# Moving the max pieces, the projections, the turned maxima and the weighted sums to other slots of a software-pipelined cross-attention

## What is computed

```python
q = (query @ Wq + bq).reshape(B, Nq, H, D).transpose(0, 2, 1, 3)        # B=32, Nq=56, H=16, D=8
k = (key_value @ Wk + bk).reshape(B, Nkv, H, D).transpose(0, 2, 1, 3)   # Nkv=1500
v = (key_value @ Wv + bv).reshape(B, Nkv, H, D).transpose(0, 2, 1, 3)
attn = jnp.einsum('bhqd,bhkd->bhqk', q, k) * scale
attn = jax.nn.softmax(jnp.clip(attn, -CLAMP, CLAMP), axis=-1)
x = jnp.einsum('bhqk,bhkd->bqhd', attn, v).reshape(B, Nq, Cq)
return x @ Wo + bo
```

## Time and profile before

| what | before |
|---|---|
| median of three runs | 974.03 us |
| profiled execution: time | 974.64 us |
| profiled execution: span | 972.5 us (2.1 us lie around it) |
| TensorE matmul busy | 924.9 us, 95% |
| VectorE / ScalarE / GpSimd busy | 699.5 / 645.9 / 351.0 us |

### The profile page before, as it was taken

The page is one execution under the profiler, slowest core; times in us unless marked ns, Lnnn a source line. Parts: engine busy times, 40 slices in busy tenths (PEclk is TensorE's granted clock), DMA queues, the critical chain, the costliest instruction groups (busy, mean ns, idle before and its releaser), DMA issues.

```text
span 972.5 us, 28783 instructions
## 1 busy us (share of the span) xinstructions
PE 924.9 (95%) x10471; PEld 741.4 (76%) x10471; DVE 699.5 (72%) x1490; ACT 645.9 (66%) x1081; POOL 351.0 (36%) x332
## 2 busy tenths in 40 slices
PE   6777999999999999999999999999999999999995
PEld 4655777777777777777777777777777778999894
DVE  6673777767676677676767767767788857777996
ACT  4654777777777777777777777777776545445554
POOL 6452362222333333222233333332222413112992
PEclk8897999999999999999999999999999999999998
DMA  5538566666655555666666555566665201002321
GB/s 141 121 79 191 120 133 140 143 136 137 137 128 119 119 119 126 141 137 138 136 137 134 119 119 119 120 137 143 137 138 111 69 1 44 23 23 86 128 114 41
DMA packets 43626, 111.44 MB, mean 115 GB/s; under 512 B 15491, under 2 KB 26053, under 8 KB 43461
## 3 DMA queue, kind: packets, MB, share of 16 engines
q1 hardware_dynamic: 43572, 110.77, 50.3%
HBM read 32.23 MB, written 1.89 MB: 35 GB/s over the span
## 4 chain that ended last, share of the span: by engine, by line
PE 84%; ACT 5%; DVE 4%; issue 3%; SPq 2%; POOL 1%; DMA 1%; ACTq 0%; DVEq 0%; POOLq 0%
PE psum L1592 17%; PE psum L1424 16%; PE psum L1652 13%; PE psum L1431 8%; PE psum L1436 8%; PE psum L1656 4%; ACT arena L759 3%; PE psum L1679 2%; PE psum L1692 2%; PE psum L1691 2%; PE psum L1680 2%; PE psum L1681 2%; PE psum L1693 2%; PE psum L1441 1%; SPq L396 1%
## 5 line engine op out<-in xcount | busy, mean ns | idle before, releaser
L946 DVE TENSOR_REDUCE arena<-psum 128x1 f32<-128x500 f32 x672 | 447.8, 674 | 210.1 <-PE psum L1424 206.9
L759 ACT ACTIVATE arena<-psum 125x896 f32<-125x896 f32 x384 | 347.5, 916 | 109.0 <-PE psum L1592 101.7
L1424 PE MATMUL psum<-K_hi,Q_bd 128*128 128x500 f32 x672 | 319.6, 485 | 7.0 <-DVE arena L946 4.1
L547 POOL TENSOR_TENSOR arena<-arena,K_hi 128x500 fp32r<-128x500 f32 x96 | 120.7, 1257 | 403.3 <-ACT K_hi L690 403.3
L1592 PEld LDWEIGHTS psum<-Q_st,K_st 97*125 97x125 f32 x1536 | 221.6, 189 | 42.4 <-ACT arena L759 16.6
L1592 PE MATMUL psum<-Q_st,K_st 97*125 97x224 f32 x1536 | 238.6, 278 | 6.1 <-ACT arena L759 5.6
L1652 PE MATMUL psum<-arena 125*25 125x168 f32 x3072 | 170.5, 311 | 0.2
L1424 PEld LDWEIGHTS psum<-K_hi,Q_bd 128*128 128x128 f32 x672 | 128.6, 192 | 53.3 <-issue 20.8
L813 ACT ACTIVATE K_st<-psum 128x448 fp32r<-128x448 f32 x128 | 69.8, 545 | 79.5 <-PE psum L1681 78.0
L1656 PE MATMUL psum<-arena 125*9 125x56 f32 x3072 | 117.6, 213 | 0.0
L1656 PEld LDWEIGHTS psum<-arena 125*9 125x9 f32 x3072 | 94.1, 91 | 16.6
(11 more groups left out here) (249 smaller groups left out, 983.3 us busy)
## 6 DMA issues: line engine op xcount, KB each, us to landing
K_st<-K_hi SPq DMA_DIRECT2D x256, 187.5 KB, 4.8
K_st<-arena SPq DMA_DIRECT2D x128, 187.5 KB, 3.4
arena<-in_ctx SPq DMA_DIRECT2D x32, 562.5 KB, 6.8
arena<-gate_rows SPq DMA_DIRECT2D x8, 896.0 KB, 4.4
arena<-in_L_ffn_W SPq DMA_DIRECT2D x16, 256.0 KB, 3.2
Q_st<-max_row SPq DMA_DIRECT2D x224, 0.5 KB, 1.7
arena<-OS_all SPq DMA_DIRECT2D x12, 168.0 KB, 4.0
x_rows<-x_all SPq DMA_DIRECT2D x1, 896.0 KB, 6.4
```

The source lines that it names most:

```text
L547: g.tensor_tensor(low.bitcast(F32R), low, K_hi[:, par, n * KB:n * KB + KB].bitcast(F32), ALU.subtract).then_inc(F["keys_low"], 1)
L759: a.activation(P2[c % NP].rearrange("p (n k) -> p n k", n=2), psum[0:CK, 2 + 2 * (c % 2):4 + 2 * (c % 2), 0:HQ // 2], ACT.Exp)\
L946: v.reduce_max(mx[:, n // NB, n % NB:n % NB + 1], bank_of(n)[:, 0:KB], AX.X).then_inc(F["piece_max_taken"], 1)
L1424: mm(bank_of(n)[:, 0:KB], Q_bd[:, par].rearrange("p h q -> p (h q)")[:, 128 * (n // NB):128 * (n // NB) + 128], K_hi[:, par, (n % NB) * KB ...
```

## The change

It writes new numbers into the slot tables and makes some of what they imply explicit. Ten pieces of batch b+2 run ahead instead of nine (`NEXT`). T moves from slot 8, behind p0, to slot 9, behind p3 and V0 (`BEFORE_TURN` = 4: p0 to p3 of batch b+2 now stand ahead of T, so the bank parity of pieces is shifted, T also waits for the maximum of p2, and p5 rather than p2 waits for `row_out`). V2 moves from slot 3 to 1, K0 to K2 from slots 5, 6, 8 to 4, 5, 6. The weighted sums move from slots 2, 5, 8, 10, 11 (2+3+3+1+3) to 3, 5, 8, 10, 11 (2+3+2+2+3). On VectorE the five steps of the softmax sums move from slots 0 to 4 to slots 3 to 5. The maxima `mx` get one buffer per parity, since p0 of the next batch now may be reduced before `row_max` has run. In the prologue four pieces of batch 1 stand ahead of `turn(0)`, and three of their maxima ahead of `row_out(0)`.

```diff
-V_SLOTS = (9, 11, 3)
-K_SLOTS = (5, 6, 8)
-SUM_SLOT, TURN_SLOT = 0, 8
-K_COPIES = (4, 6, 7)
...
+V_SLOTS = (9, 11, 1)
+K_SLOTS = (4, 5, 6)
+COPY_SLOT, SUM_SLOTS, SCALE_SLOT = 0, (3, 3, 4, 5), 5
+ROW_SLOT, TURN_SLOT, KEEP_SLOT = 7, 9, 9
+V_COPIES = (9, 11, 2)
+K_COPIES = (3, 5, 6)
+NEXT, BEFORE_TURN = 10, 4
...
         def bank_of(n):
 
-            return bank[0 if n == 0 else (n + 1) % 2]
+            return bank[(n + (n >= BEFORE_TURN) + 1 + BEFORE_TURN) % 2]
...
-            row_max(0)
+            row_max(0, 0)
+            for n in range(BEFORE_TURN - 1):
+                piece_max(1, 1, n)
             row_out(0)
-            for n in range(3):
-                piece_max(1, n)
+            for n in range(max(BEFORE_TURN - 1, 0), BEFORE_TURN + 2):
+                piece_max(1, 1, n)
...
-                if n == 2:
+                if n == BEFORE_TURN + 1:
                     if turns:
                         pe.wait_ge(F["max_row_ready"], b + PRIME)
...
-            def turn(b):
+            def turn(b, more):
 
                 pe.wait_ge(F["row_max_taken"], b + 1 + PRIME)
+                if more and BEFORE_TURN > 1:
+                    pe.wait_ge(F["piece_max_taken"], (b + 1) * PIECES + BEFORE_TURN - 1 + PRIME)
...
-            pieces1(0)
-            turn(0)
-            pieces1(1)
+            pieces1(*range(BEFORE_TURN))
+            turn(0, True)
+            pieces1(BEFORE_TURN)
```

More of the change, by code:

```diff
@@ L329, in pieces @@
         def pieces(c, table):
-            return [(2 if n < 9 else 1, n) for n in table.get(c, ())]
+            return [(2 if n < NEXT else 1, n) for n in table.get(c, ())]
         def bank_of(n):
-            return bank[0 if n == 0 else (n + 1) % 2]
+            return bank[(n + (n >= BEFORE_TURN) + 1 + BEFORE_TURN) % 2]
         def has(b, ahead):
@@ L749, in period @@
                 for c in range(NC):
-                    if c == 0 and has(b, -1):
+                    if c == COPY_SLOT and has(b, -1):
                         act.wait_ge(F["outputs_made"], b * NC + PRIME)
@@ L760, in period @@
                          .then_inc(F["weights_ready"], 1)
-                    if c == 9 and has(b, 1):
+                    if c == KEEP_SLOT and has(b, 1):
                         keep_extremes(b + 1)
@@ L988, in _, with taken @@
             v.memset(bank[6], 0.0).then_inc(F["bank_cleared"], 1)
-            for n in range(3, 9):
-                piece_max(1, n)
-            def taken(b, c, table):
+            for n in range(BEFORE_TURN + 2, NEXT):
+                piece_max(1, 1, n)
+            def taken(b, par, c, table):
                 for ahead, n in pieces(c, table):
@@ L995, in taken @@
                         continue
-                    piece_max(b + ahead, n)
+                    piece_max(b + ahead, (par + ahead) % 2, n)
             def period(b, par, half):
                 for c in range(NC):
[L1000 to L1003, removed]
+                    taken(b, par, c, EARLY_PIECES)
+                    taken(b, par, c, MID_PIECES)
+                    if c == ROW_SLOT and has(b, 1):
+                        row_max(b + 1, 1 - par)
                     if c == TURN_SLOT and has(b, 1):
@@ L1534, in _, with bank_free @@
             last.then_inc(w_ps, 1)
-            pieces1(2, 3)
+            pieces1(*range(BEFORE_TURN + 1, BEFORE_TURN + 3))
             pe.wait_ge(F["keys_copied"], 2 * NB + PRIME)
             value_project(1, 0)
-            pieces1(4, 5, 6, 7)
+            pieces1(*range(BEFORE_TURN + 3, NEXT - 1))
             pe.wait_ge(F["values_copied"], NB + 1 + PRIME)
             value_project(1, 1)
-            pieces1(8)
+            pieces1(NEXT - 1)
+            def bank_free(b, kind, n):
+                if isinstance(b, int) and b == B - 2:
+                    pe.wait_ge(F["keys_copied"], B * NB + PRIME)
+                    pe.wait_ge(F["values_copied"], B * NB - 1 + PRIME)
+                    return
+                i = [p[1:] for p in PROJECTIONS].index((kind, n))
+                if isinstance(b, int) and b == 0 and i == 0:
+                    pe.wait_ge(F["values_copied"], NB + 2 + PRIME)
+                _, last, m = PROJECTIONS[i - 1]
+                batch = 1 if last == "values" and m == 2 else 2
+                pe.wait_ge(F[f"{last}_copied"], b * NB + ((batch - (i == 0)) * NB + m + 1) + PRIME)
             def max_scores(b, par, c, table):
@@ L1624, in period @@
                         n = V_SLOTS.index(c)
-                        if n == 0:
-                            pe.wait_ge(F["keys_copied"], (b + 3) * NB + PRIME)
-                        else:
-                            pe.wait_ge(F["values_copied"], b * NB + (ahead * NB + n) + PRIME)
+                        bank_free(b, "values", n)
                         value_project((par + ahead) % 2, n)
```

66 lines of the change are left out of this document (32 added, 34 removed).

## The result

The changed kernel is slower: 993.72 us in the median of four runs (991.71 to 999.82) against 974.50 of the kernel before (972.60 to 975.99, four runs), a ratio of 1.021 (95% interval 1.016 to 1.026). I had forecast 985 (974 to 993): the direction is right, the size is 9 us short and just outside the range. The profiled execution is the longest of the four, 999.82 us with a span of 998.0, so its spans hold some 6 us more than the median.

A forecast was written before the change was run, and what follows sets the result against it. TensorE's own order was taken to bound the steady loop. Loop +1.5, slow row DMAs +2.5, start +4.5 and end +2.5 summed to +11 on a profiled 974.64: 985.6, or 985 us for the median, range 974 to 993.

The forecast's parts named there:

- The wait goes: -0.44: Steady period, S2: its wait for exponential 0 vanishes because S1, p10, V2 and p11 stand behind S0; -0.44 us a period.
- I count the exchanges as 0. A period without waits is then 21.7: TensorE's work per period: moved sums and pieces cost nothing net, so 22.16 - 0.44 = 21.7 us.
- From T to S0 ... = 5.82: Steady period: TensorE's work between T and S0 falls from 8.64 to 5.82 us.
- The chain is ... 6.13, and about 0.05 until TensorE goes on: 6.18: Steady period: T, row_out and seven row DMAs through landing take 6.13 us, 6.18 until TensorE goes on.
- S0 waits for the row in every period, 0.36: Steady period: the 6.18 us chain exceeds 5.82 us of work, so S0 waits 0.36 us.
- 22.21 against 22.16: Steady period, new against old: +0.05 us in each of some 27 periods, +1.5 us in all.
- Periods whose row DMAs are slow: +2.5: Straight-code periods 2 to 4 and 30: slower DMA issue lengthens the wait, 0.65 us each; +2.5 us.
- The start ... +4.5: Prologue: row_out(0), the queue and K0's copy come 2.3 us later, S0 of period 1 at 106.5 against 101.96; +4.5 us.
- The end ... +2.5 (0 to 4): Period 30 and the next phase: less work from T to S0, row DMAs delay the last period's S0; +2.5 us.
- Rival A: Loop: the row stays hidden and S2's gain stands, 10 us faster there, 970 us in all; chance 0.1.
- Rival B: Loop: new waits on VectorE of paired pieces p14/p15, p16/p17, p4/p5 add 0.2 us a period, 990 us; chance 0.2.
- Rival C: Start: worse than counted, clock late by a step and ScalarE's queue behind K0's copy, 988 us; chance 0.15.

The follow-up runs named there:

- f3: The kernel before with V2 alone moved from slot 3 to 1 and its copy from 3 to 2: 972.49 us, ratio 0.999.
- e3: The changed kernel with one DMA for the seven rows, same data, place and order: 976.24 us, ratio 1.0036.
- e2: The changed kernel with T(0) and row_out(0) in the prologue moved up, behind one piece instead of four: 995.76 us, ratio 1.023.
- e4: The changed kernel with VectorE's gathers of periods 28 to 30 in slots 0, 1, 11 instead of 2, 4, 7: 991.45 us, ratio 1.020.
- g3: The changed kernel with one row DMA and the gather steps in slots 0, 1 and 11: 973.88 us, ratio 0.999.
- f1: The changed kernel with T ahead of V0 instead of behind it, within slot 9: 986.82 us, ratio 1.014.
- f2: The kernel before with one row DMA instead of seven: 973.29 us, ratio 0.998.
- g1: The kernel before with T alone moved to slot 9 behind p0 to p3, with the changed kernel's bank parity, waits and prologue: 1028.82 us, ratio 1.054.
- g2: The changed kernel with one row DMA and the softmax sums on VectorE back in slots 0 to 4: 976.77 us, ratio 1.003.

## Why the prediction was right in direction and short in size

The sum had +11 us, the three stretches that count took +20.3. Nearly all that was short lies in two terms. The loop: +1.5 was said for 27 periods at +0.05, and the steady periods took +0.27, 5.8 us more. The end: +2.5 and one slow row of 0.65 were said for periods 28 to 30, and they took +8.6, 5.5 us more. The start and the slow rows were 1 us each too high. In the sum's own words:

- **"The wait goes: -0.44"**: right, S2 has none in after. f3 shows that this is worth only 0.07 in the old layout, since the next wait stands behind it.
- **"I count the exchanges as 0. A period without waits is then 21.7"**: wrong by 0.34. e3 shows it at 22.04. About two thirds of that is at T. Before, T and the three sums behind it took 1.47 (403.49 to 404.96), where three sums alone take 1.28, so T cost 0.19 and S10 0.44; in e3 T takes 0.31 (488.50 to 488.81) and S10 behind it 0.53, together 0.21 more. The values are most of the rest: eight value matmuls cost 0.79 ahead of a piece, but 0.97 ahead of T (504.32 to 505.29) and 0.96 ahead of sums (508.60 to 509.56). The piece that lost its place behind them was itself dearer there, 0.31 behind V0 and 0.40 behind V1, than between other neighbours, 0.24. So V0 with its piece went from 1.10 to 1.21 and V1 with its piece from 1.19 to 1.20. The other exchanges do come out near 0.
- **"From T to S0 ... = 5.82"**: 6.12 in e3, though the count of sums behind T was off by one (seven before, not six; the 0.89 taken away for two of them is right). 0.12 of the 0.30 is T, 0.18 is V1, which had been taken at 0.79.
- **"The chain is ... 6.13, and about 0.05 until TensorE goes on: 6.18"**: this is the first step that failed: the wait is there as said, and its chain is 0.27 longer. Measured 6.41 and 6.50. `row_out` ends 0.80 behind T instead of 0.70; issue and landing take 5.46 instead of 5.4; and from landing to S0 it is 0.12 and 0.20 by turns instead of 0.05. The prologue's row, from which I took 0.70, has T behind one piece; here T is behind V0.
- **"S0 waits for the row in every period, 0.36"**: right, 6.45 - 6.12 = 0.33. Both terms were 0.3 too small, so that the wait came out right is luck, and the period did not. **"S0 to T ... 16.03"**: 15.97 in the mean. **"22.21 against 22.16"**: 22.43 in the steady periods. 0.27 x 27 = 7.3 us where I had 1.5.
- **"Periods whose row DMAs are slow: +2.5"**: the total is about right, the places are not. Over the steady 6.45, T to S0 was longer in period 2 (7.29, so 0.84) and in 28 and 29 (7.32 and 6.84, so 0.87 and 0.39): 2.1 in all. Of the four periods to which I gave 0.65 each it was one; in period 30 T to S0 was 6.39.
- **"The start ... +4.5"**: +3.5. The copy of K0 was to be 2.3 later and S0 of period 1 at 106.5; they came at 88.12 (before 84.83) and 107.08, of which 1.6 is the later `row_max(0)`. From `row_max(0)` to the end of `row_out(0)` the step was 4.2 in my sum and 4.14 in the trace. e2 shows that 1.0 of the 3.5 goes back if `row_out(0)` is put 1.33 us earlier; the rest is the last 0.9 us of its position, order and clock, which I didn't separate. The stall and the half clock in this term are those of the earlier trace rows, the queue is SyncE's in the start.
- **"The end ... +2.5 (0 to 4)"**: the second step that failed, +8.6 for periods 28 to 30, where I had that and 0.65. The row's part was right, 3.3 (e3). What I put at nothing is the rest: 3.6 for the order and VectorE's work of that phase, which stands in e3 without any wait for the row, and 1.6 to 1.7 that goes with the half clock in period 30. Most of the 3.6 stays open. The gathers are a part: S0 to T is 16.93 (713.60 to 730.52) where steady periods have 15.97. Timelines of VectorE and GpSimd in after:

```profile
721.73 1.25 POOL L550 TENSOR_TENSOR arena<-arena,K_hi 128x500 fp32r<-128x500 f32 x1 [9.64 <-ACT K_hi L693]
722.06 1.40 DVE L914 SCALAR_TENSOR_TENSOR OS_all<-OS_all,slot_rows 128x448 f32<-128x448 f32 x1
726.85 1.26 POOL L550 TENSOR_TENSOR arena<-arena,K_hi 128x500 fp32r<-128x500 f32 x1 [0.67 <-ACT K_hi L693]
727.04 1.54 DVE L916 SCALAR_TENSOR_TENSOR OS_all<-OS_all,slot_rows 128x448 f32<-128x448 f32 x1
```

and the same two steps in before, where only the second meets a step of GpSimd:

```profile
707.47 0.68 DVE L911 SCALAR_TENSOR_TENSOR OS_all<-OS_all,slot_rows 128x448 f32<-128x448 f32 x1
712.66 1.25 POOL L547 TENSOR_TENSOR arena<-arena,K_hi 128x500 fp32r<-128x500 f32 x1 [2.40 <-ACT K_hi L690]
713.00 1.39 DVE L913 SCALAR_TENSOR_TENSOR OS_all<-OS_all,slot_rows 128x448 f32<-128x448 f32 x1
```

A step takes 0.68 us alone. If it starts while GpSimd's 1.25 us step runs, it is through about half a microsecond after that one ends: 722.06 + 1.40 = 723.46, and GpSimd ended at 722.98. GpSimd's steps follow the key copies, which moved a slot up, and now meet both. All four steps shown here agree, and so do those of every run: 0.67 or 0.68 us alone, 1.39 to 1.56 where they start during such a step of GpSimd. In e4 and g3 none does, and all six take 0.67 or 0.68. There moving the steps away makes a period up to 0.6 us shorter (0.6 and 0.2 in g3) and hands most of it to the third. How much of that is GpSimd and how much the queue of sums and pieces on VectorE, these runs don't separate.

The rivals:

- **Rival A** (row hidden) is refuted by the rows of S0. It would have needed T ahead of V0 (f1), and then the gain would be none: 22.23, not 21.8. **Rival B** (pieces wait for VectorE in the new pairs) is there, 17.6 us of weight-load waits for 18 periods against 8.3, but e3 has the same 17.6 and a period below before's, so it isn't what made after slow; how much of the 22.04 it holds stays open. **Rival C** (a worse start) did not come.

What remained of the gain: with the DMA chain out of the way the layout is 0.12 a period better than before (3.3 us), about 2 worse in the start (e3 40.4 against f2 38.2) and 3.6 worse at the end (68.85 against 65.26). That is g3 and e3, 0.999 and 1.004.

## What to carry to other kernels

Before moving the instruction that starts a serial chain (transposition, copy, DMAs), compare the chain, hand-overs included, with the work left between it and its consumer. If the two are within half a microsecond, each 0.1 us counts once per period. The better remedy here was a shorter chain: one DMA for seven gave back 17 of 19 us, T ahead of V0 7, T in slot 8 about 11. And price the last periods apart from the loop: three of them cost as much as the other 27 here. On an engine that is saturated, a wait taken away at one instruction counts only after the next wait behind it has been looked at: 0.44 became 0.07 here. Price an operation together with its neighbours, not by its kind, and both ends of an exchange: what leaves a place was priced by that place too.

## What the runs showed of the hardware

- Seven DMAs of 0.5 KB on SyncE's queue took 5.46 us from the first issue to the last landing in the steady periods (before, after); one DMA for the same 3.5 KB took 1.86 (e3, f2).
- TensorE's granted clock, 1.00 throughout the steady loop of before and after, fell to 0.5 for some 3.4 us at 370, 513 and 656 us in g1, whose TensorE stood still for up to 0.9 us at S0 in each period (14.9 us in 17 periods). One such stretch costs 1.5 us: S0 to T was 18.54 in the period from 511.37, 17.0 in the others.
- The half-clock stretches between S0 of period 31 and TensorE's last matmul lasted 0 to 10.2 us in runs of almost the same order. I found no rule for them, and at half speed 10.2 us are 5 us of the span (an estimate). One that falls into a stretch that is compared, as in period 30 of after and of g2, looks like a cost of the change: 1.6 and 1.7 us for 3.4 us at half clock.
- A step of VectorE with two inputs in SBUF (128x448) took 0.67 or 0.68 us alone and 1.39 to 1.56 where it started during a 1.25 us step of GpSimd, over all runs; it ended 0.48 or 0.49 behind that one.
